# A graph-and-mixing block on one core: graph logits placed behind the mix weight's low parts, and chunk 1's rows and turned rows loaded at other times

## The reference

```
gnn:  xt = xn @ weight                      (4 heads of 64)
      alpha = softmax(leaky_relu(alpha_l[src] + alpha_r[dst]))      over the heads
      tmp[n] = sum over heads of alpha[n] * xt[dst[n]]     for the first 6250 edges
      out = tmp in each of the four heads
mix:  q, k, v = xn @ w_qkv + b;  k, v = layernorm by head
      kv = sum over all rows of k v^T / 6250;  ret = q kv + xn
      h = gelu(ret @ w1 + b1);  mix = h @ w2 + b2 + xn
x  <- x + gnn(xn) + mix(xn)
ffn:  xn2 = layernorm(x);  w = softmax(xn2 @ Wr + br)      (8 experts)
      y_e = relu(bn(relu(bn(xn2 @ W1_e)) @ W2_e)) @ Wo_e + bo_e
x  <- x + sum over e of w_e y_e
```

## Time and profile before

| | us |
|---|---|
| median of 3 runs | 1104.76 (1102.22 to 1104.92) |
| the profiled execution's own time | 1105.07 |
| its span, first to last instruction | 1103.2 |
| PE busy | 1091.8 (99%) |
| DVE, ACT, POOL busy | 751.4, 735.4, 244.8 |

### The profile page before, as it was taken

How to read it: one execution, slowest core, us unless ns; L and a number is a source line. 1 busy time by engine, 2 the same in 40 slices (tenths; PEclk the granted TensorE clock), 3 DMA queues, 4 the chain that set the end, 5 groups by cost and what they waited for, 6 DMA issues and landing times.

```text
span 1103.2 us, 19336 instructions
## 1 busy us (share of the span) xinstructions
PE 1091.8 (99%) x6656; PEld 978.3 (89%) x6656; DVE 751.4 (68%) x1752; ACT 735.4 (67%) x1275; POOL 244.8 (22%) x274
## 2 busy tenths in 40 slices
PE   9999998999999999999999999999999999999998
PEld 7988988989888888888898888888888988889998
DVE  7887756776576675775765766757757657666565
ACT  5787747675676766756756757666667567566665
POOL 4887753312012021030120120210301201100000
PEclk9999999999999999999999999999999999999999
DMA  6989970111011110110110111101101101100000
GB/s 190 256 221 254 250 194 21 59 34 54 1 49 48 39 46 14 39 59 1 49 49 1 49 49 39 49 10 40 59 1 49 49 7 37 34 20 1 1 20 15
DMA packets 78326, 67.82 MB, mean 61 GB/s; under 512 B 27667, under 2 KB 73605, under 8 KB 78229
## 3 DMA queue, kind: packets, MB, share of 16 engines
q1 hardware_dynamic: 73438, 59.35, 19.5%
q0 software_dynamic: 3968, 6.61, 2.3%
q10 hardware_dynamic: 823, 0.64, 0.3%
HBM read 40.77 MB, written 25.80 MB: 60 GB/s over the span
## 4 chain that ended last, share of the span: by engine, by line
PE 90%; POOL 3%; issue 2%; DVE 2%; DMA 1%; ACT 1%; SPq 0%; DVEq 0%; ACTq 0%; POOLq 0%
PE bank L280 28%; PE bank L282 28%; PE bank L281 28%; POOL gathered L596 1%; PE bank L977 1%; PE bank L1156 1%; PE bank L1144 1%; PE bank L1154 1%; DMA node_alpha_l<-residual 1%; PE bank L918 1%; PE bank L910 0%; DMA node_alpha_l<-gathered 0%; PE bank L1172 0%; POOL gathered L611 0%; POOL ffn_w_low L603 0%
## 5 line engine op out<-in xcount | busy, mean ns | idle before, releaser
L1373 DVE SCALAR_TENSOR_TENSOR accumulated<-bank,router_w,accumulated 128x256 f32<-128x256 f32 (+2 forms) x392 | 170.2, 478 | 199.4 <-PE bank L282 192.8
L652 ACT ACTIVATE h<-weight_stage 128x512 fp32r<-128x512 f32 (+2 forms) x206 | 113.6, 599 | 197.1 <-PE bank L282 177.7
L282 PE MATMUL bank<-ffn_w_high,h 128*128 128x256 f32 (+2 forms) x778 | 220.0, 283 | 0.0
L280 PE MATMUL bank<-ffn_w_high,h 128*128 128x256 f32 (+2 forms) x778 | 219.6, 282 | 0.2 <-DVE h L1223 0.2
L281 PE MATMUL bank<-ffn_w_low,h 128*128 128x256 f32 (+2 forms) x778 | 219.8, 283 | 0.0
L1223 DVE TENSOR_TENSOR h_low<-activated,h_high 128x512 fp32r<-128x512 f32 (+2 forms) x208 | 135.2, 657 | 79.5 <-ACT h_high L652 75.8
L804 ACT ACTIVATE activated<-bank,bn_cols 128x512 f32<-128x512 f32 (+2 forms) x208 | 156.3, 752 | 48.1 <-PE bank L282 45.0
L804 ACT ACTIVATE weight_stage<-bank,bn_cols 128x512 f32<-128x512 f32 (+2 forms) x208 | 154.3, 750 | 47.5 <-PE bank L282 46.7
L611 POOL DMA_INDIRECT gathered<-node_table,indices x49 | 61.0, 1244 | 516.9 <-DVE residual L1430 499.0
L280 PE MATMUL bank<-xT_high,ffn_w_high 128*128 128x512 f32 (+2 forms) x416 | 159.6, 384 | 0.1
L280 PE MATMUL bank<-h_high,ffn_w_high 128*128 128x512 f32 (+2 forms) x416 | 157.8, 379 | 0.0
(11 more groups left out here) (225 smaller groups left out, 1877.5 us busy)
## 6 DMA issues: line engine op xcount, KB each, us to landing
x_rows<-in_x SPq DMA_DIRECT2D x18, 512.0 KB, 5.6
x_turned<-xT_high SPq DMA_DIRECT2D x22, 256.0 KB, 5.0
x_turned<-xT_low SPq DMA_DIRECT2D x22, 256.0 KB, 7.0
out<-accumulated SPq DMA_DIRECT2D x11, 512.0 KB, 3.3
mix_xT_high<-x_turned SPq DMA_DIRECT2D x10, 512.0 KB
mix_xT_low<-x_turned SPq DMA_DIRECT2D x10, 512.0 KB
weight_stage<-in_L_ffn_W SPq DMA_DIRECT2D x16, 256.0 KB, 5.0
node_table<-gathered SPq DMA_DIRECT2D x22, 130.0 KB, 4.0
```

The source lines that it names most:

```text
L280: nc.tensor.matmul(dst, ah, bh, start=(k == 0), stop=False)
L282: last = nc.tensor.matmul(dst, al, bh, start=False, stop=(k == n - 1))
L652: return nc.scalar.activation(dst, src, ACT.Copy)
L1373: last = V.scalar_tensor_tensor(a, y_of(ch, e)[b][0:tp, (t % 2) * D:(t % 2 + 1) * D], wts(ch)[0:tp, t, e:e + 1], a, ALU.mult, ALU.add)
```

## The change

Two of the edits are in SP's order, two in DVE's.

```diff
@@ sync: in the loop over the first pass's tiles
                 if i == 38:
                     load_turned(CHUNKS[0])
+                if i == NTILES - 5:
+                    load_turned(CHUNKS[1])
                 if i == NTILES - 2:
                     need(sp, s["xnorm"], NTILES)
                     load_rows(CHUNKS[0])
             store_turned(pair_ahead(NTILES - 4))
-            load_turned(CHUNKS[1])
+            need(sp, s_gath[0], gathered(CHUNKS[0]))
             load_rows(CHUNKS[1])
@@ vector: the turn between the passes
             copy(Pm[:, 0, :], KVb[1][:, 0:D]).then_inc(s["m_pv"], 1)
-            logits(CHUNKS[0])
             for k in range(KT):
                 dve.wait_ge(s["m_hi"], k + 1)
                 low(mwl[:, 0, k, :], KVb[2 + k][:, 0:D], mwh[:, 0, k, :]).then_inc(s["m_lo"], 1)
...
-            for step in (weigh, gel_low, add_messages, x2, x2_norm, x2_low):
+            for step in (logits, gel_low, weigh, add_messages, x2, x2_norm, x2_low):
                 step(CHUNKS[0])
```

## The result

| | before | changed |
|---|---|---|
| median of 10 runs each, us | 1104.74 (1102.22 to 1105.89) | 1106.99 (1105.59 to 1107.83) |
| profiled execution, own time and span | 1105.07, 1103.2 | 1106.96, 1105.1 |
| PE busy | 1091.8 | 1094.6 |

The changed kernel is slower: ratio 1.0023, 95% interval 1.0014 to 1.0032, some 2.3 us. Both of its medians, 1106.99 and 1106.19, lie above the predicted range's 1105.2, and the sign is the other one.

The account below looks back on a forecast made before the run. PE bounds the kernel, so only its gaps in the turn count. `x2_turn` coming 1.7 us earlier, all else at nothing, takes the span from 1103.2 to 1101.5, own time 1103.4, median 1103.1 us; range 1100.8 to 1105.2.

Parts of the forecast that it names:

- The bound: PE is busy 1091.8 of 1103.2 us; only its gaps, about 5 us, nearly all in the turn between passes, can move.
- `mix1` began without a wait: In PE's turn, `mix1` was to begin at 164.25 instead of 166.39, 2.1 us earlier.
- POOL is late next: In the turn, POOL's four gathers for chunk 1 hold `norm2` until 172.35, making POOL late by 0.4 us.
- landing in time: Chunk 0's gathers land by 164.45, when DVE finishes the bias column; forecast landing 164.0, so nothing is lost.
- where I had 1.7: Norm chain on POOL and DVE: `norm2`, and with it `x2_norm` and `x2_turn`, come 1.7 us earlier.
- where I had 1.6: PE's gap ahead of `x2_turn` was to grow from 0.37 to about 1.6 us.
- Such a gather lands in 2.29 us when the DMA engines are quiet: Chunk 0's last gather: issue to landing bounded by 2.3 and 5.35 us, taken as 2.3 plus 0.1.
- The rows of chunk 1: Issued behind the gathers at 164.0, landing 5.6 us later at 169.6; a start on ACT by 170.3 costs nothing.
- the start of the gathers: On POOL, the early load delays the start by 0 to 3.1 us, taken as 1.8, to 157.5.
- rival 1: Table stores held up the whole 3.1 us, gathers land at 165.3, gain 0.9 or less: 1104.0; chance 0.20.
- chunk 0's rows "at nothing": Issued 1.1 us later behind 1 MB; ACT hides 1.2 us and DVE 0.4 to 0.5 us of delay.
- My rival on the slow side: Table stores held up 3.1 us, gathers still needing 5.35 us, `x2_turn` 2.0 us later: 1106.8; chance 0.08.

Follow-up runs that it names:

- kernel 4: The change without its early load (both DVE moves, chunk 1's rows held), against the kernel before: 1104.14 us, ratio 0.9985.
- kernel 6: Both DVE moves, chunk 1's rows held, turned rows at the old place, 15 instead of 9 idle products, against before: 1103.26 us, ratio 0.9988.
- kernel 12: Both DVE moves and chunk 1's rows held, no early load, measured again on another chip against before: 1103.68 us, ratio 0.9990.
- kernel 3: Only chunk 1's rows held until chunk 0's gathers land, all else as in the kernel before: 1104.30 us, ratio 0.9976 against before.
- kernel 9: The changed kernel with one 512 KB part of the turned rows at tile 44, the other at the old place: 1104.84 us, ratio 1.0011 against before.
- kernel 10: Both DVE moves, chunk 1's rows held, two 4 KB DMAs at tile 44 in place of the early load: 1103.85 us, ratio 0.9991 against before.
- kernel 2: Only chunk 1's turned rows loaded early, at tile 44, all else as in the kernel before: 1108.64 us, ratio 1.0017 against before.
- kernel 5: The changed kernel with 17 instead of 9 idle products ahead of `x2_turn`: 1104.76 us, ratio 1.0000 against before.
- kernel 1: Only the DVE moves, SP as in the kernel before: 1105.03 us, ratio 0.9993 against before.
- kernel 8: The changed kernel itself, measured again beside others on their chip: 1106.19 us, ratio 1.0012 against before.
- kernel 7: The changed kernel with its early load one tile earlier, behind tile 42's table store: 1108.58 us, ratio 1.0041 against before.

## Why the prediction was wrong

**Right.** The bound: of the spans' difference all but the start's luck arose in the turn. `mix1` began without a wait, and "POOL is late next": `norm2` follows POOL's fourth gather at once, in the changed kernel and in kernels 4, 6 and 12. With landing in time, as the sum assumed, `x2_turn` comes 2.0 us earlier (kernel 4) where I had 1.7, behind a gap of 1.5 where I had 1.6. "Such a gather lands in 2.29 us when the DMA engines are quiet": it took 2.31 with a DMA share of at most 0.38 (164 to 168), and 2.51 in kernel 3 with at most 0.28 (162 to 165). The rows of chunk 1 landed 3.9 us behind their issue where I took 5.6; they came 1.17 us after ACT wanted them, and the cover of over 2 us hid it.

**Wrong, first: the start of the gathers.** "Moves by between 0 and 3.1 us. I take 1.8": it was 3.5, outside my bounds. I had taken the load's price as its bytes at the best rate seen, less what the quiet engines before it could take in. They took in nothing, because the load's data did not flow until over 2 us behind its issue. So the gathers had landed at 8.15 us from the turn's start, where 6.6 was the last that cost nothing: these 1.5 us are what is missing between the 1.7 forecast for `x2_turn` and the 0.24 measured. This is rival 1, past its price. Kernels 9 and 10 show that both parts of my sum are in it, SP's issues with about 1.3 us of delay and the slower landing of the stores with 1.65; the issues alone cost nothing.

**Wrong, second: chunk 0's rows "at nothing".** The cover was rightly read (1.2 us and 0.4 to 0.5), but ACT got them 2.6 us later than before, counted from the turn's start. That put 0.95 us on PE at the turn's first product; in kernels 2 and 5 2.7 us. In the changed kernel's profile the gather's chain was later still and hid it; in kernel 5's it set the turn.

**Wrong, third: the clock.** The sum has no term for it. In the profile of before the granted clock stayed full through the gap of 2.21 us and behind it (1.00 in every window from 164 to 201), and the sum made the new gap 1.6. The gap became 2.25 us, since the late landing held up the chain to `x2_turn` by 1.5 us and the late rows held up PE by only 0.95, and the clock fell: 1.4 us in this profile, 0.9 of it net of the hidden wait, and 3.8 net in those of kernels 1 and 8. Kernel 5 measures it: 1.4 us of the median come back when the gap is filled, and the kernel is level with before. In the profiled pair the first error takes the gain away and this one makes the loss; over all executions the estimate above gives about half of the loss to the clock. The profile of before is of an execution without a fallen clock in the turn, and by the means two of three executions of before have one: even a gap that was there already isn't safe on the word of one profile.

My rival on the slow side (the gathers late and still 5.35 us under way, 1106.8) came out near the median by another road, and is no merit: the gathers landed fast.

Why the last store landed 7.07 us behind its issue, and 5.42 without the load, was not settled. The DMA engines were full meanwhile (a share of 0.92 to 1.20 in the windows from 152 to 159); the expectation of kernel 7 sets an order of landings beside the engines' time, and no run here separates the two.

## What to carry to other kernels

A load that is moved earlier is not free because its own consumer has time: list every transfer that now stands behind its bytes, and who waits for those; here holding a load back until an urgent small one had landed was worth 1.2 to 1.9 us (kernels 3, 4 and 12 against before), and pulling another forward cost 1.5 to 2.6 (kernel 5 against 6, kernel 2 against before). When an edit on a side engine takes waits away from PE, ask where PE will wait instead, and whether several short gaps become one: removed waits that meet in one place can cost more than they did apart, as the stretches of 10.2 us at half clock show, which only the kernels with a gap of 2.2 to 2.6 us ahead of `x2_turn` have. (Kernel 7, where PE stands ahead of the turn, has means down to 0.992.) If PE must wait there anyway, products that nobody reads are a cheap filling: eight of them brought 1.4 us in kernel 5, six in kernel 6 nothing that can be measured. And look at the granted clock of all executions before reading a gap as harmless from one profile.

## What the runs showed of the hardware

- Behind gaps of much the same length PE's clock stayed full or not, from execution to execution of one kernel. After 2.2 to 2.6 us (before, kernels 1, 8 and 9, and the changed one) it was at half (0.50) for 0, 3.4 or 10.2 us; while PE stood for 3.28 us (kernels 2 and 5) it fell before the gap was over, and was at half for 3.4 and 6.8 us. After 1.5 us or less no profiled execution showed a fall, though 10 of 57 executions of kernels 3, 4, 6, 10 and 12 have a mean that is the sign of one. Why the same gap ends differently was not settled.
- A load of 1 MB from DRAM, issued to nearly idle DMA engines at 146.76, moved next to nothing until past 149 (4 to 5 GB/s in 147 to 149); then the engines ran at 373 to 406 GB/s, over the 359 that I had taken for the most (the trace of before has 369 in its window from 7 to 8 us).
- The first 16 products of the kernel took 5.23 to 6.78 us, a difference of up to 1.55 us from execution to execution, while the granted clock read 1.00. A comparison of two single profiles has to take that off first.
